# A state space scan with its B and C tables in SBUF, PSUM banks in pairs, and its output sums finished on ScalarE and POOL

## What is computed

```
phi = cumsum(dt) * rope_freqs            # angles, one per state pair
B, C = rope(rms(Braw) + B_bias, phi), rope(rms(Craw) + C_bias, phi)
h_t = exp(-exp(A_log)*dt_t) * h_{t-1} + (x_t*dt_t) B_t^T ;  y_t = h_t C_t
```

## Time and profile before

| what | us |
|---|---|
| median of three runs | 2638.09 |
| the profiled execution, its time | 2641.73 |
| its span from first to last instruction | 2639.7 |
| the scan in it: first product of VectorE to last output | 203.0 to 1473.6 |
| a step of the scan, inside it | 19.7 |

### The profile page before, as it was taken

The page is one execution under the profiler, slowest core; times in us unless marked ns, Lnnn a source line. Parts: engine busy times, 40 slices in busy tenths (PEclk is TensorE's granted clock), DMA queues, the critical chain, the costliest instruction groups (busy, mean ns, idle before and its releaser), DMA issues. The chain is left out here.

```text
span 2639.7 us, 61136 instructions
## 1 busy us (share of the span) xinstructions
PE 2154.0 (82%) x19761; PEld 1590.8 (60%) x19761; DVE 1937.0 (73%) x5279; ACT 1543.8 (58%) x3098; POOL 1486.5 (56%) x2287
## 2 busy tenths in 40 slices
PE   8946888888888888878887799786799767758887
PEld 5634655565655665655655588565355445548887
DVE  4538999999999999999999444466333267747776
ACT  5657898999899999999897122355122112212222
POOL 2447787888788788888787222244111144414444
PEclk9976898988898888998897799888899878879999
DMA  5766666666666666666675367343222233321110
GB/s 171 245 193 175 163 167 174 173 176 174 161 169 180 168 176 175 168 174 175 161 183 142 108 204 233 128 139 124 77 84 84 71 103 116 117 69 37 48 48 28
DMA packets 295374, 373.58 MB, mean 142 GB/s; under 512 B 44852, under 2 KB 234871, under 8 KB 295127
## 3 DMA queue, kind: packets, MB, share of 16 engines
q1 hardware_dynamic: 285254, 343.10, 47.0%
q0 software_dynamic: 9872, 27.28, 3.1%
HBM read 151.03 MB, written 85.00 MB: 89 GB/s over the span
## 5 line engine op out<-in xcount | busy, mean ns | idle before, releaser
L667 POOL TENSOR_TENSOR p_CR<-p_pc 128x256 f32<-128x256 f32 x512 | 373.3, 729 | 189.5 <-DVE p_pc L991 165.9
L671 POOL TENSOR_TENSOR p_BR<-p_pb 128x256 f32<-128x256 f32 x512 | 373.4, 729 | 26.5
L748 PE MATMUL p_ps_sc<-p_CR,p_BR 64*128 64x128 f32 x4096 | 341.6, 313 | 54.8 <-DVE p_M L1004 32.9
L748 PEld LDWEIGHTS p_ps_sc<-p_CR,p_BR 64*128 64x128 f32 x4096 | 289.6, 213 | 113.9 <-issue 86.4
L881 ACT ACTIVATE p_D<-p_ps_x 128x512 f32<-128x512 f32 x512 | 289.5, 593 | 109.5 <-PE p_ps_x L714 108.8
L1004 DVE TENSOR_TENSOR p_M<-p_ps_sc,p_D 128x512 f32<-128x512 f32 x512 | 327.9, 680 | 29.7 <-PE p_ps_sc L748 28.9
L991 DVE SCALAR_TENSOR_TENSOR p_pc<-p_ps_c,p_beta,p_cs 128x256 f32<-128x256 f32 x512 | 243.0, 475 | 46.8 <-DMA p_sn<-p_tr_s 31.3
L763 PE MATMUL p_ps_y<-p_M,p_uexp 128*32 128x128 f32 x4096 | 259.7, 282 | 0.0
L991 DVE SCALAR_TENSOR_TENSOR p_pc<-p_ps_c,p_beta,p_sn 128x256 f32<-128x256 f32 x512 | 242.6, 474 | 0.0
L997 DVE SCALAR_TENSOR_TENSOR p_pb<-p_ps_b,p_beta,p_cs 128x256 f32<-128x256 f32 x512 | 242.5, 474 | 0.0
L997 DVE SCALAR_TENSOR_TENSOR p_pb<-p_ps_b,p_beta,p_sn 128x256 f32<-128x256 f32 x512 | 242.5, 474 | 0.0
(11 more groups left out here) (277 smaller groups left out, 5293.4 us busy)
## 6 DMA issues: line engine op xcount, KB each, us to landing
p_cs<-p_tr_c SPq DMA_DIRECT2D x256, 256.0 KB, 4.1
p_sn<-p_tr_s SPq DMA_DIRECT2D x256, 256.0 KB, 4.5
p_phib<-scratch_phi SPq DMA_DIRECT2D x256, 128.0 KB, 3.1
p_x<-scratch_rt SPq DMA_DIRECT2D x72, 128.0 KB, 2.0
scratch_ro<-p_o POOLq DMA_DIRECT2D x72, 128.0 KB, 2.0
p_xT<-in_xT SPq DMA_DIRECT2D x64, 128.0 KB, 4.6
scratch_u<-p_u SPq DMA_DIRECT2D x16, 512.0 KB, 3.8
scratch_wu<-p_wu SPq DMA_DIRECT2D x16, 512.0 KB, 4.3
```

Of the source, the lines that this page charges most:

```text
L667: e.tensor_tensor(CR[:, p, g, :], pc[:, g % 2, 0, :], pc[:, g % 2, 1, :], ALU.add).then_inc(S["rotC"], 1)
L671: e.tensor_tensor(BR[:, p, g, :], pb[:, g % 2, 0, :], pb[:, g % 2, 1, :], ALU.add).then_inc(S["rotB"], 1)
L748: m = e.matmul(sc_ps[half][:, (g * 2 + b) * L:(g * 2 + b + 1) * L], BR[half * 64:half * 64 + 64, p, 2 * q + g, b * L:(b + 1) * L], CR[half ...
```

## The change

- `c_ps` and `b_ps` go. `bc` has two buffers in SBUF, and `products` read the tables from there. In place of `held_bc` one ScalarE instruction per chunk puts the sign on two tables in place, in the third step of a chunk.
- The four free banks make `x_ps` two pairs of banks. `exponents` fills one pair while ScalarE empties the other, one `decays` takes a pair (128x1024), `turned` takes half a step's B at a time. `sc_ps` is one pair, and one `decayed` on VectorE multiplies 128x1024.
- Whole turns, magnitudes and sines on ScalarE are merged into fewer, longer instructions.
- `outputs` leaves VectorE. ScalarE copies the whole bank `y_ps` into `y` (`sums_out`), after the third `decays` call of a step, and POOL scales and adds in SBUF at the end of its step.
- Constants used only at the start now lie in the `y` tile.

```diff
-        bc = sb("bc", [P, 4, CT])
+        bc = sb("bc", [P, 2, 4, CT])
...
-        yx = sb("yx", [P, 2, CT])
-        y = sb("y", [P, 2, CT])
-
-        c_ps, b_ps, y_ps, ns_ps = (ps(n) for n in ("c", "b", "y", "ns"))
-        x_ps = [ps(f"x{i}") for i in range(2)]
-        sc_ps = [ps(f"sc{i}") for i in range(2)]
+        y = sb("y", [P, 2, 2, CT])
...
+        y_ps, ns_ps = (ps(n) for n in ("y", "ns"))
+        x_ps = [ps2(f"x{i}") for i in range(2)]
+        sc_ps = ps2("sc")
...
+            order += [("D", t, 1)] + [("B", t - 1, 1)] * kept + [("D", t, 2), ("D", t, 3)] + [("S", t - 2)] * (2 <= t < LAST + 2)
+            order += [("B", t, 0)] * (t < LAST) + [("D", t + 1, 0)] * (t + 1 < T)
... SyncE
             def load_bc(c):
-                at_least(e, S["bcp_ok"], c, 4, 0)
+                at_least(e, S["prodC"], c, 2 * NG * NB, -2 * NG * NB)
+                at_least(e, S["prodB"], c, 2 * NG * NB, -2 * NG * NB)
... POOL
+            def outputs(t, p):
+                at_least(e, et_in[p], t - p, 8, 16)
+                at_least(e, S["y_ev"], t, 1, 1)
+                e.tensor_tensor(y[:, p, 1, :], y[:, p, 1, :], et[:, p, :], ALU.mult).then_inc(S["yx_ok"], 1)
+                at_least(e, S["yx_ok"], t, 1, 1)
+                e.tensor_tensor(y[:, p, 0, :], y[:, p, 0, :], y[:, p, 1, :], ALU.add).then_inc(S["y_ok"], 1)
...
                         for b in range(BATCH):
                             stage_u(t, p, g // 2, b)
+                    if g == 7 and t:
+                        outputs(t - 1, 1 - p)
... TensorE
-                at_least(e, S["x_ok"], i, 1, 0)
-                bank = [x_ps[(i + half) % 2] for half in range(2)]
+                at_least(e, S["x_ok"], i, 1, -1)
+                bank = [x_ps[i % 2][:, half, :] for half in range(2)]
... ScalarE
+            def signed_bc(c):
+                at_least(e, S["bc_in"], c, 96, 96)
+                e.activation(bc[:, c % 2, 1:4:2, :], bc[:, c % 2, 1:4:2, :], ACT.Copy, scale=sign[:, :]).then_inc(S["bcp_ok"], 1)
...
+            def sums_out(t, p):
+                at_least(e, S["yi_mm"], t, U, U)
+                at_least(e, S["yx_mm"], t, U, U)
+                if t >= 2:
+                    at_least(e, y_out[p], t - p, 8, 0)
+                e.activation(y[:, p, :, :], y_ps[:, :].rearrange("p (a n) -> p a n", a=2), ACT.Copy).then_inc(S["y_ev"], 1)
...
-                e.activation(D[:, n, :], x_ps[i % 2][:, :], ACT.Exp).then_inc(S["x_ok"], 1)
+                e.activation(D[:, 2 * q:2 * q + 2, :], x_ps[i % 2][:, :, :], ACT.Exp).then_inc(S["x_ok"], 1)
... VectorE
-                    e.scalar_tensor_tensor(out=pc[:, g % 2, n - 2, :], in0=c_ps[:, (n - 2) * CT:(n - 1) * CT], scalar=beta[:, k, n, g:g + 1],
+                    e.scalar_tensor_tensor(out=pc[:, g % 2, n - 2, :], in0=bc[:, c % 2, n, :], scalar=beta[:, k, n, g:g + 1],
                                            in1=tr[:, p, g % 2, g // 2, :], op0=ALU.add, op1=ALU.mult).then_inc(S["prodC"], 1)
...
-                    e.scalar_tensor_tensor(out=pb[:, g % 2, n, :], in0=b_ps[:, n * CT:(n + 1) * CT], scalar=beta[:, k, n, g:g + 1],
+                    e.scalar_tensor_tensor(out=pb[:, g % 2, n, :], in0=bc[:, c % 2, n, :], scalar=beta[:, k, n, g:g + 1],
                                            in1=tr[:, p, g % 2, g // 2, :], op0=ALU.add, op1=ALU.mult).then_inc(S["prodB"], 1)
...
-                e.tensor_tensor(M[:, m_slot(p, n), :], sc_ps[n % 2][:, :], D[:, n, :], ALU.mult).then_inc(S["m_ok"], 1)
+                m = m_slot(p, n)
+                e.tensor_tensor(M[:, m:m + 2, :], sc_ps[:, :, :], D[:, n:n + 2, :], ALU.mult).then_inc(S["m_ok"], 2)
```

More of the change, by code:

```diff
@@ L555, in expand @@
                 p = k % 2
-                used, ready = count(e, t, 2 * NG, -2 * NG), count(e, t, 2, 2)
+                used, ready = count(e, t, 2 * NG, -2 * NG), count(e, t, 1, 1)
                 if not (isinstance(t, int) and t < 2):
@@ L689, in _ @@
                 step(T - NB + k, k, NC - 1)
+            outputs(T - 1, 1)
         @block.tensor
@@ L879, in decays @@
+            def decays(t, q):
+                i = place["D", t, q]
                 at_least(e, S["x_mm"], i, 1, 1)
[L880 to L884 removed]
+                at_least(e, S["m_ok"], t, U, 2 * q + 2 - U)
+                e.activation(D[:, 2 * q:2 * q + 2, :], x_ps[i % 2][:, :, :], ACT.Exp).then_inc(S["x_ok"], 1)
@@ L885, in turned @@
+            def turned(t, h):
+                i = place["B", t, h]
                 at_least(e, S["x_mm"], i, 1, 1)
                 at_least(e, S["ns_mm"], t, NQ, 0)
[L887 to L918, removed]
-                if t < LAST:
-                    turned(t, 0)
-                if t + 2 < T:
-                    magnitude(t + 2, p, 1)
-                if t + 1 < T:
-                    decays(t + 1, 0)
-                    decays(t + 1, 1)
-                if t + 2 < T:
-                    sines(t + 2, p)
-                if t < LAST:
-                    turned(t, 1)
-                if ahead:
-                    in_turns(t + 3, (k + 3) % NB, 3)
-                    whole_turns(t + 3, (k + 3) % NB, 3)
@@ L942, in own, with step @@
                         return bass.AP(tensor=ap.tensor, offset=ap.offset, ap=[list(ap.ap[0]), [2 * P + 16, 2], [32, BATCH * NQ], [1, HD]])
-                    e.activation(own(ST[r, t % NB, 0, 0, h * HD:h * HD + HD]), own(x_ps[i % 2][r, h * HD:h * HD + HD]), ACT.Copy
+                    e.activation(own(ST[r, t % NB, 0, 0, h * HD:h * HD + HD]), own(x_ps[i % 2][r, 0, h * HD:h * HD + HD]), ACT.Copy
                                  ).then_inc(S["x_ok" if h else "kept"], 1)
+            def step(t, k, c):
+                p = k % 2
+                ahead, s3, k3 = t + 3 < T, t + 3, (k + 3) % NB
+                decays(t, 1)
+                if ahead:
+                    in_turns(s3, k3, 0)
+                    near_turns(s3, k3, 0)
+                if t and t <= LAST:
+                    turned(t - 1, 1)
+                if ahead:
+                    in_turns(s3, k3, 1)
+                decays(t, 2)
+                if t:
+                    sums_out(t - 1, 1 - p)
+                if ahead:
+                    near_turns(s3, k3, 1)
+                    whole_turns(s3, 0)
+                decays(t, 3)
+                if k == 2 and c + 1 < NC:
+                    signed_bc(c + 1)
+                if ahead:
+                    in_turns(s3, k3, 2)
+                    near_turns(s3, k3, 2)
+                if 2 <= t < LAST + 2:
+                    state(t - 2)
+                if t < LAST:
+                    turned(t, 0)
+                if t + 2 < T:
+                    magnitude(t + 2, p)
+                if t + 1 < T:
+                    decays(t + 1, 0)
+                if t + 2 < T:
+                    sines(t + 2, p)
+                if ahead:
+                    in_turns(s3, k3, 3)
+                    near_turns(s3, k3, 3)
+                    whole_turns(s3, 1)
             def all_turns(s):
@@ L952, in _ @@
                 if s == 0:
-                    held_bc(0)
-                for v in range(2):
-                    magnitude(s, s, v)
+                    signed_bc(0)
+                magnitude(s, s)
                 sines(s, s)
-            for n in range(2):
-                decays(0, n)
+            decays(0, 0)
             all_turns(2)
@@ L966, in _ @@
                 step(T - NB + k, k, NC - 1)
+            sums_out(T - 1, 1)
         @block.vector
@@ L1034, in step @@
                         decayed(t, p, 2 * q - 2)
-                        decayed(t, p, 2 * q - 1)
                     elif later:
                         decayed(t - 1, 1 - p, U - 2)
-                        decayed(t - 1, 1 - p, U - 1)
                         if 2 <= t < LAST + 2:
                             new_state(t - 2, p, (k + 2) % NB)
-                    if q == 2 and later:
-                        outputs(t - 1, 1 - p)
             for k in range(NB):
@@ L1050, in _ @@
             decayed(T - 1, 1, U - 2)
-            decayed(T - 1, 1, U - 1)
-            outputs(T - 1, 1)
 def norm_names():
```

139 lines of the change are left out of this document (58 added, 81 removed).

## The result

The changed kernel takes 2993.91 us (median of four runs, 2993.57 to 2995.29) against 2638.27 us in the same session: a ratio of 1.134, with a 95% interval of 1.131 to 1.137. Forecast were 2982 us, between 2850 and 3110.

The account below looks back on a forecast made before the run. VectorE was taken to bound the scan's 19.7 us step; turns with POOL raise it to 25.1, so 5.4 us times 64 is 343, plus 1 for prologue and end: 2982 us as a median, range 2850 to 3110.

Parts of the forecast that it names:

- VectorE sets the step: Scan of the kernel before: VectorE, 96% busy with 0.7 us of waits, bounds the 19.7 us step.
- the second SBUF operand decides: Products in the scan: reading both tensors from SBUF makes them take turns with POOL, 0.47 us lost per POOL instruction among them.
- products with a median well over 474 ns: Sign that the forecast is right: scan products get this median and a longest of 0.85 to 1.1 us.
- The price of a turn: VectorE product and POOL add in the scan: 0.86 us for both, of which VectorE loses 0.47.
- the rival on the faster side: Scan products take no turns because of their per-partition scalar; POOL bounds at 19.0 us a step, 2593 us; chance 0.04.
- the one in which the whole instruction is exclusive: Rival: no part of contending scan instructions overlaps, turn 1.20 us, step of 30 us, 3300 us; chance 0.04.
- The walk through a quarter: VectorE's quarter step: three POOL adds cost 0.47 us each and L658 0.2, giving 5.87 us, four quarters 23.5.
- The outputs: Moved to POOL at g = 7, among products: 2 x 0.47 = 0.94 us a step more for VectorE.
- State: VectorE's two state instructions, with one SBUF tensor: add 0.78 us a step and cover 0.2.
- VectorE's own waits: Waits of 0.7 us a step mostly vanish in the longer step; 0.1 kept, range 0 to 0.7.
- The multiplications' gain of 0.28 us a step: VectorE: four 128x1024 multiplications replace eight of 512, saving a 0.07 us gap per pair.
- The other queues at no cost: ScalarE at most 18.5 us a step, TensorE 16.7, both hidden under 25; loads and stores on SyncE cost nothing.

Follow-up runs that it names:

- 1: Kernel before with only the B and C tables moved to two SBUF buffers that the products read: 2970.5 us, ratio 1.123.
- 2: Kernel before with only the B tables in SBUF, C tables still in PSUM: 2828.0 us, ratio 1.072.
- 3: Changed kernel with POOL's sums into CR and BR replaced by memsets, which write SBUF but read nothing: 2603.4 us, ratio 0.986.
- 4: Changed kernel with the outputs back on VectorE's third quarter, reading PSUM: 2967.6 us, ratio 1.124.
- 10: Kernel before with VectorE's multiplications merged, ScalarE's whole turns, magnitudes and sines merged, and outputs moved to ScalarE and POOL: 2586.2 us, ratio 0.980.
- 5: Kernel before with only the outputs moved from VectorE to ScalarE and POOL: 2649.0 us, ratio 1.002.
- 8: Kernel before with only VectorE's multiplications merged to 128x1024, tables in PSUM: 2646.0 us, ratio 1.001.
- 11: Kernel before with only ScalarE's whole turns, magnitudes and sines merged: 2595.7 us, ratio 0.981.
- 9: Kernel before with VectorE's multiplications merged and ScalarE's whole turns, magnitudes and sines merged, outputs on VectorE: 2576.2 us, ratio 0.977.
- 6: Changed kernel with tables back in PSUM and one pair of x banks, wide instructions and moved outputs kept: 2676.9 us, ratio 1.011.

## Why the prediction was right

- **VectorE sets the step, and the second SBUF operand decides.** Shown by 1, 2 and 3: the tables alone cost 12.3%, half of them 7.2%, and beside memsets no product is stretched. The sign "products with a median well over 474 ns" held for two of the four kinds (938 and 944 ns); the other two keep 473 and 475, since by the walk only some products of a quarter wait.
- **The price of a turn**, 0.86 us for both and 0.47 for VectorE, taken from the earlier trace rows at another width and another operation, measured 0.87 and 0.48 (0.87 less 0.39). The products, with their per-partition scalar, take the same turns, so the rival on the faster side had no ground; nor had the one in which the whole instruction is exclusive (0.47 and 0.73, 1.20 us a turn). The Trainium skill says of the one that starts first, in "SBUF — State Buffer", "SBUF: two separate sides", that it "gets the pair for the whole instruction". The trace agrees in that the other waits, but not to the full length: 0.33 of the 1.20 us overlap, the two times 0.15 us of the earlier trace rows and little more. What passes in them no run shows.
- **The walk through a quarter** gave three sums and 0.2 us of L658 and 5.87 us. Measured are the same three products (the fourth, sixth and eighth), `M` at 1.13 us, 0.25 us for L666, and 5.96. Four times 0.09, or 0.36 us a step, was lacking; the terms of the next point gave 0.14 back. So the forecast step was 25.1 us and the measured one is 25.3 (1000 us over 158/4, from 600 to 1600), and the 12 us between forecast and result are smaller than the walk's own error of 23.
- **The outputs** at 0.94 us: 0.96 (6.92 less 5.96). State: 0.6 against 0.54 (6.50, from 915.05 to 921.55, less 5.96). VectorE's own waits: 0.1 against none.
- **The multiplications' gain of 0.28 us a step** is in the walk (`M` at 1.12 us), and most of it is lost again there, since the walk lets L658 outlast `M`. That was right, and it means that the merge by itself brings next to nothing: all the wide instructions together (1 against 4, in different sessions) are worth 3 us, and not 18. In two quarters of four what leaves `M` comes back as waiting for L666; in the quarters with the state and with the outputs 0.06 us each is left (6.50 against 6.56).
- **The other queues at no cost**: TensorE and ScalarE have gaps everywhere, as expected, and from 600 to 1600 us VectorE waits for nothing.
- **The kernel without turns**, which the rival on the faster side had at 19.0 us a step and 2593 us, was not run as it is: its wide instructions and the tables in PSUM would take ten banks, where both kernels use eight. The nearest is 10, with ScalarE's merges: 19.0 us (800 us over 168/4) and 2586 us. But that kernel's gain isn't that of VectorE's fewer instructions, by which the prediction reasoned: 5 and 8 took 0.78 and 0.28 us a step off VectorE, and nothing came of it while ScalarE's queue was as before. "VectorE sets the step" was thus only nearly true of the kernel before; the forecast didn't depend on it, since in the changed kernel VectorE is alone.

## What to carry to other kernels

Where VectorE is the bound and POOL works out of SBUF beside it, an operand in PSUM is worth a bank: moving four tables of 256 columns out of two banks cost 12% of this kernel's time. An engine at 96% with its few waits spread over every step isn't yet alone in setting the time; here fewer instructions on its neighbour came first, and only then did fewer of its own bring anything. Price a wait between two engines from any pair of rows that shows it, in both directions, and walk one period: the count of collisions matters as much as their price.

## What the runs showed that was not expected

- In the kernel before, 0.28 us a step off VectorE brought nothing (8), the merges on ScalarE 47 us (11), both 65 us (9), each against the kernel before beside it (2642.65 and 2640.95).
- The order of the two engines locks into one pattern: in experiment 2 all 281 second B products from 500 to 1300 us are stretched (mean 946 ns), and the first ones are not (470). In the changed kernel the quarters keep their lengths too, 5.96 us or near it wherever no state or outputs come in.
- The granted clock from 300 to 1300 us (1 would be 2.4 GHz throughout) is 0.82 in the changed kernel, 0.88 before and 0.98 in 9, with 9056, 11588 and 12171 matmuls. The number of matmuls alone doesn't give it: 6 has 0.91 with 11096. What sets it stays open; the changed kernel's time doesn't hang on it, since VectorE has no gap there.
